# Attention in four layers: context products of a key tile made once over 512 columns, in place of twice over 256

## The reference, cut to what matters

```python
q = heads(hidden_states @ Wq + bq)
k = heads(hidden_states @ Wk + bk)
v = heads(hidden_states @ Wv + bv)
...
attn = jnp.einsum('bhqd,bhkd->bhqk', q, k) * scale
attn = jax.nn.softmax(attn.astype(jnp.float32), axis=-1).astype(q.dtype)
ctx = jnp.einsum('bhqk,bhkd->bhqd', attn, v)
ctx = ctx.transpose(0, 2, 1, 3).reshape(B, N, D)
return ctx @ Wo + bo
```

## Time and profile before

| | us |
|---|---|
| median of 3 runs | 3119.75 |
| lowest and highest | 3117.68, 3122.37 |
| profiled execution, its own time | 3117.75 |
| its span from first to last instruction | 3116.0 |
| TensorE busy | 2592.7 |
| VectorE busy | 2327.4 |
| ScalarE busy | 1901.9 |
| GpSimd busy | 1453.0 |

### The profile page before, as it was taken

How to read it: one execution, slowest core, us unless ns; L and a number is a source line. 1 busy time by engine, 2 the same in 40 slices (tenths; PEclk the granted TensorE clock), 3 DMA queues, 4 the chain that set the end, 5 groups by cost and what they waited for, 6 DMA issues and landing times. The chain is left out here.

```text
span 3116.0 us, 43575 instructions
## 1 busy us (share of the span) xinstructions
PE 2592.7 (83%) x15639; PEld 970.1 (31%) x15642; DVE 2327.4 (75%) x2851; ACT 1901.9 (61%) x3284; POOL 1453.0 (47%) x2030
## 2 busy tenths in 40 slices
PE   7799999997469759999999834877777778998777
PEld 3122222222146412222222224622222323443233
DVE  6899999995136469999999661268999996556567
ACT  3599999995024239999999702475555553325444
POOL 4666666650635356666666116615777773000000
PEclk9799999998689869999999957987999999999799
DMA  4111111106322331111111212111000000331000
GB/s 129 42 26 27 27 30 28 27 19 139 46 68 68 86 99 27 27 26 27 26 26 29 90 42 80 57 58 40 7 7 14 7 7 1 94 99 40 1 0 28
DMA packets 171154, 134.05 MB, mean 43 GB/s; under 512 B 67474, under 2 KB 141586, under 8 KB 170682
## 3 DMA queue, kind: packets, MB, share of 16 engines
q1 hardware_dynamic: 133978, 92.04, 11.3%
q0 software_dynamic: 36800, 39.15, 4.5%
q10 hardware_dynamic: 160, 0.07, 0.0%
HBM read 80.80 MB, written 45.93 MB: 41 GB/s over the span
## 5 line engine op out<-in xcount | busy, mean ns | idle before, releaser
L774 DVE TENSOR_REDUCE a_att_mx<-a_att_s 128x2 f32<-128x1024 f32 x960 | 1118.9, 1217 | 90.5 <-PE a_att_s L649 88.3
L753 ACT ACTIVATE a_att_pt<-a_att_st 128x512 f32<-128x512 f32 x2048 | 1085.2, 604 | 73.9 <-PE a_att_st L678 58.6
L678 PE MATMUL a_att_st<-a_qst,a_kst 50*128 50x512 bf16 x2048 | 650.9, 385 | 5.0 <-ACT a_att_pt L753 1.8
L665 PE MATMUL a_att_av<-a_att_pt,a_att_vst 128*32 128x256 f32 (+1 forms) x7168 | 628.9, 423 | 8.3
L649 PE MATMUL a_att_s<-a_kst,a_qst 48*128 48x512 bf16 x2048 | 584.1, 396 | 61.5 <-PEq L312 32.0
L2373 POOL TENSOR_TENSOR g_xn<-m2s_hs,m2s_cb 128x1024 f32<-128x1024 f32 x128 | 300.8, 2355 | 118.9 <-DVE m2s_hs L2340 64.3
L678 PEld LDWEIGHTS a_att_st<-a_qst,a_kst 50*128 50x128 bf16 x2048 | 152.1, 94 | 546.5 <-ACT a_att_pt L753 454.9
L2340 DVE TENSOR_TENSOR_SCAN m2s_hs<-m2s_da,m2s_bps 128x1024 f32<-128x1024 f32 x128 | 292.7, 2287 | 4.4
L665 PEld LDWEIGHTS a_att_av<-a_att_pt,a_att_vst 128*32 128x32 f32 x7168 | 143.1, 108 | 329.0 <-ACT a_att_pt L753 199.0
L530 POOL TENSOR_TENSOR g_area<-g_area 128x512 f32<-128x512 f32 (+3 forms) x256 | 177.9, 695 | 144.0 <-ACT g_area L744 128.9
L2256 PE MATMUL m2s_yps<-g_xn,g_ident 128*128 128x512 f32 x512 | 243.0, 597 | 0.9
(11 more groups left out here) (482 smaller groups left out, 3822.2 us busy)
## 6 DMA issues: line engine op xcount, KB each, us to landing
f_share<-f_comb_rows SPq DMA_DIRECT2D x128, 128.0 KB, 3.0
a_qst<-a_qstk POOLq DMA_DIRECT2D x124, 64.0 KB, 2.3
a_kst<-a_kstk POOLq DMA_DIRECT2D x124, 64.0 KB, 2.4
f_xs<-f_sent SPq DMA_DIRECT2D x20, 396.0 KB, 6.2
a_qstk<-a_qkv_part SPq DMA_DIRECT2D x16, 384.0 KB, 3.6
f_sent<-f0r_zero SPq DMA_DIRECT2D x1, 5148.0 KB, 22.4
a_kstk<-a_qkv_part SPq DMA_DIRECT2D x32, 128.0 KB
a_kstk<-a_qkv_part SPq DMA_DIRECT2D x16, 256.0 KB
```

The source lines that it names most:

```text
L665: mm = pe.matmul(av[32 * gr:32 * gr + 32, at], vst[u][:, kt, h, :], pt[:, 4 * (kt % 4) + 2 * half + h, at], start=kt == 0, stop=kt == 7)
L678: pe.matmul(st[:, e % 3, :], kst[u][64 * h:64 * h + STACK, kt * P:(kt + 1) * P], qst[u][64 * h:64 * h + STACK, half * CH:(half + 1) * CH], ...
L753: act.activation(pt[:, e % 16, :], st[:, e % 3, :], ACT.Exp, scale=scale).then_inc(exp_done, 1)
L774: dve.tensor_reduce(mx[:, par, 2 * cut:2 * cut + 2], s1[:, cut % 2, :, :], AX.X, ALU.max).then_inc(s1_used, 1)
```

## The change

`weigh` loses its `part`. Every key tile is weighed once, with all 512 columns, after the fourth score of the round. For tiles 1 to 6 the two calls of half the columns become one; for tiles 0 and 7 the call moves from behind the second score to behind the fourth. At the end of the stage, tiles 6 and 7 are weighed whole, as tile 7 was before.

```diff
-                def weigh(n, u, kt, part):
-                    if kt == 0 and part == 0:
+                def weigh(n, u, kt):
+                    if kt == 0:
                         pe.wait_ge(vcopied, n + 1)
                         if not (isinstance(n, int) and n < 1):
                             pe.wait_ge(evac, n)
                     pe.wait_ge(exp_done, UNITS * n + 4 * kt + 4)
-                    if kt in (0, 7) and part == 1:
-                        return
-                    at = slice(part * CH // 2, (part + 1) * CH // 2) if 0 < kt < 7 else slice(0, CH)
                     for half in range(2):
                         for h in range(2):
                             gr = 2 * h + half
-                            mm = pe.matmul(av[32 * gr:32 * gr + 32, at], vst[u][:, kt, h, :],
-                                           pt[:, 4 * (kt % 4) + 2 * half + h, at], start=kt == 0, stop=kt == 7)
+                            mm = pe.matmul(av[32 * gr:32 * gr + 32, :], vst[u][:, kt, h, :],
+                                           pt[:, 4 * (kt % 4) + 2 * half + h, :], start=kt == 0, stop=kt == 7)
...
                             scores(n, u, kt, (2 * half,), before)
                             cut(half)
                             scores(n, u, kt, (2 * half + 1,), before)
-                            if kt >= 2:
-                                weigh(n, u, kt - 2, half)
-                            elif before:
-                                weigh(n - 1, (u + 3) % 4, kt + 6, half)
+                        if kt >= 2:
+                            weigh(n, u, kt - 2)
+                        elif before:
+                            weigh(n - 1, (u + 3) % 4, kt + 6)
...
                 project(0)
-                weigh(NPAIR - 1, 3, 6, 0)
-                weigh(NPAIR - 1, 3, 6, 1)
+                weigh(NPAIR - 1, 3, 6)
                 project(1)
-                weigh(NPAIR - 1, 3, 7, 0)
-                weigh(NPAIR - 1, 3, 7, 1)
+                weigh(NPAIR - 1, 3, 7)
```

## The result

The changed kernel takes **3209.47 us** (3200.05 to 3214.42, 4 runs) against 3121.06 us (4 runs of the kernel before beside it): a ratio of **1.0277, 95% interval 1.0248 to 1.0307**. It is slower by 88 us. Its profiled execution took 3207.6 us, with a span of 3205.9 against 3116.0.

A forecast was written before the change was run, and what follows sets the result against it. TensorE narrowly bounds the kernel before; afterwards the 2.39 us loop through three score banks does. 29 steady pairs at +1.16 us plus head and tail give 39.2 a stage, 78.4 for both: 3117.75 + 78.4 = 3196 us, range 3160 to 3235.

The forecast's parts named there:

- The bound before, TensorE by little: Mid-stage of the first attention stage, kernel before: TensorE bounds, busy 494.71 of 500 us, against VectorE 466.70 and ScalarE 474.19.
- TensorE's saving, 0.22 us a round: Rounds with merged tiles 1 to 6: TensorE needs 2.00 us instead of 2.22, 1.3 us less a pair if never waiting.
- The turn of 2.39 us: Plain round's loop from exponential through score, whole product and next score to exponential: 0.65 + 0.32 + 1.00 + 0.42 us.
- Round 1, 3.04 us: Second round of a pair: the copy of products waits for tile 7's later product, so the round takes 3.04 us.
- The pair, 20.23 us: Steady head pair of eight rounds: 6 x 2.39 + 3.04 + 2.85 = 20.23 us against 19.07, +1.16 us.
- The clock: TensorE's clock expected to stay 1.00; a fall to 1.2 GHz throughout would add 650 us, within a rival given 0.05.
- The rest: Each stage's head and tail: last two pairs +2.5 and +2.4 us, first pair +0.7; VectorE and GpSimd costed at nothing.
- TensorE's saving arrives: Rival: scores run far enough ahead to cover 1.00 us; pair 17.6 to 17.8 us, -1.3 a pair, total 3038; chance 0.06.
- Only the floor: Rival: ScalarE's idle 0.43 us a round swallows both copies, 3130 us, or 3156 if only round 1's excess vanishes; chance 0.06.
- No matter at all: Rival: halves and whole products cost the same on both paths, so time stays at 3118 us; chance 0.03.
- VectorE's late cuts: Part of the slower-still rival: 0.1 us more lost each round in mid-stage, +50 us, 3246 us; rival's chance 0.05.

The follow-up runs named there:

- v1: Kernel before, with score banks numbered through all pairs instead of restarting at bank 0 each pair: 3075.50 us, ratio 0.9956 to the kernel before.
- e2: Kernel before, with both unmerged halves of tiles 1 to 6 side by side behind the fourth score, tiles 0 and 7 whole there: 3200.46 us, ratio 1.0262.
- e1: Changed kernel, with every whole product moved from behind the fourth score to behind the second: 3212.21 us, ratio 1.0304 to the kernel before.
- x3: Changed kernel, with the first pass multiplying only one head's scores, still three score banks: 3205.32 us, ratio 1.0277 to the kernel before.
- x4: Same as x3 (one head's first-pass scores), but with four score banks: 3092.13 us, ratio 0.9914 to the kernel before.
- e6: Same as e1 (whole products behind the second score), with score banks numbered through all pairs: 3141.42 us, ratio 1.0169 to the kernel before.
- e5: Kernel before, with only tiles 1 to 6 merged, whole behind the fourth score; tiles 0 and 7 stay behind the second: 3187.62 us, ratio 1.0225.
- h1: Kernel before, with only tile 2's product merged, whole behind the fourth score of round 4: 3139.61 us, ratio 1.0064 to the kernel before.

## Why the prediction was right

The forecast was 3196 us, the range 3160 to 3235, and the likeliest case was the one that came. Point by point:

- *The bound before, TensorE by little.* Right but incomplete. v1 shows that the turn already bound the kernel before once a pair, for 0.2 us. The prediction said that no row before shows a gap in mid-stage; it had counted with a wait for exponential e - 3 everywhere and overlooked the restart.
- *TensorE's saving, 0.22 us a round.* It never arrives, as said. Its size was read from rows of before and no run shows it apart. The prediction spoke of the changes of weights in front of and behind a product; e2, which saves the same changes without any wider matmul, holds TensorE for the same 1.00 us and so leaves the width no part in it.
- *The turn of 2.39 us.* Right to the hundredth in the profile, in e1 and in x3. That it is counted against the exponentials that the banks hold is what x4, e6 and v1 show.
- *Round 1, 3.04 us.* The copy waits for the late product: idle 0.53 us in each of 30 pairs. e1 and e5 took the wait away.
- *The pair, 20.23 us.* It was 20.30. Three of the seven hundredths are in round 1, 3.07 for 3.04: the copy comes 2.10 us behind exponential 4 and not 2.08, and exponential 7 follows it by 0.49 and not 0.47. Two are in rounds 4 and 5, which take 2.83 and 2.43 for 2.85 and 2.39, since the exponentials run 0.64 for 0.60 us behind the long copy. Over 58 steady pairs that is 4 us of the gap.
- *The clock.* This step failed. I had argued from a stage that keeps 1.00 at 78.90 busy in 100 that it wouldn't fall; a last pair is busy 15.07 in 19.37 us where the clock stays, about the same share, and it fell in the second stage in both profiles of this kernel. The mechanism was among the rivals, but priced for whole stages and not for one pair. It is 9.0 us of the profiled execution's 90, and most of the 11.5 between forecast and profile.
- *The rest.* The last two pairs of the first stage cost 2.56 and 2.41 us, as forecast. The first pairs cost 0.7 and 1.2 us, for 0.7 each. Everything else together, most of it outside the attention stages, is 2.3 us shorter than before, which the sum had at nothing; it hides that much of the gap.

Of the rivals, *TensorE's saving arrives* asked for a turn under 2.22 us, and the turn is 2.39. x4 shows the other way to get there, a turn that covers one exponential more; its pair of 18.54 us stays above the rival's 17.6 to 17.8, even with half the cut matmuls left out. Of the rule of the Trainium skill beside it (Perfetto Trace Analysis, Optimizing Tensor Performance, Matmuls), that larger matmuls are more efficient, this kernel's runs show no gain for 512 against 256 columns: 1.00 us for either in e2. *Only the floor* fell with the copy's 0.53 us of waiting, *No matter at all* with the ratio of 1.0277. *VectorE's late cuts* didn't come: VectorE lost work in mid-stage, 445.79 us for 466.70, and the turn kept its 2.39.

The experiments' own misses were e1 (a wait not read in the listing), h1 (a saving counted where TensorE was waiting), and e2 and x4, by 0.3 us a pair each.

## What to carry to other kernels

Before joining two pieces of work on a shared in-order engine, follow the turn that goes through the buffers: from the consumer's start back to its next feed, with the joined piece in it. Set it against the work that the consumer has in that time: the piece it has just begun and one for each buffer. Here that is four exponentials, 4 x 0.49 = 1.96 us with three banks, against 0.65 + 0.42 us of latencies and 0.32 + 1.00 of interruption, 2.39, however much total work the join saves. With half the product the turn was 1.96, and it fitted. And look where the buffer numbering restarts: an index modulo 3 that begins anew every 32 steps gives away a buffer each time. Whether that costs anything depends on what stands there: 14 us in the kernel before, nothing in the changed one.

## What the runs showed of the hardware that I had not expected

- Two adjacent groups of 256 columns and one of 512 keep TensorE equally long, 1.00 us: these float32 products with 32 output columns gain nothing from 512 columns in place of 256. What splitting them costs is the change to the scores and back, 0.22 us for the one pair of changes that a round saves, worked out from rows 4 and 5 of the kernel before.
- With equal instructions, and equal busy time up to the fall (4.10 and 4.09 of 5.93 us), the last pair ran at clock 1.00 in the first attention stage and fell to 0.50 in the second, in both profiles of this kernel (0.62 and 0.61 over the pair).
